# x of batch 2 ahead of the last rows, w2 behind the rows of batch 1, and matmuls into free banks: a cross-attention and feed-forward kernel on one core

## The reference

```
LQ, LKV, HID, H, G = 256, 256, 512, 32, 8      # head size 16, 4 query heads for each of 8 key heads
n = layernorm(x)
q = n @ Wq.T + bq;  k = ctx @ Wk.T + bk;  v = ctx @ Wv.T + bv
scores = q . k / sqrt(16), masked to -inf by a causal_mask argument and by padding
x = x + (softmax(scores) @ v) @ Wo.T + bo
f = layernorm(x)
h = gelu(silu(bitlinear158(f, w1, b1)))         # 512 -> 2048
h = layernorm(h) * ln_g + ln_b
x = x + bitlinear158(h, w2, b2)                 # 2048 -> 512
```

## Time and profile before

| | |
|---|---|
| median of 3 runs | 617.34 us (617.25 to 619.74) |
| the profiled execution | 618.85 us |
| its span, first to last instruction | 616.8 us |
| granted TensorE clock, mean | 0.933 |
| PE, DVE, ACT, POOL busy | 516.5, 490.3, 351.9, 137.9 us |
| moved by DMA | 72.17 MB, 117 GB/s over the span |

### The profile page before, as it was taken

One profiled execution on the slowest core, in us unless ns is written; L12 is line 12 of the kernel. 1 busy time (PEld: TensorE's weight loads), 2 busy tenths in 40 slices (PEclk: granted clock), 3 DMA queues, 4 the chain that ended last, 5 costly groups with the idle time before them and its releaser, 6 DMA issues.

```text
span 616.8 us, 8915 instructions
## 1 busy us (share of the span) xinstructions
PE 516.5 (84%) x3374; PEld 284.2 (46%) x3374; DVE 490.3 (79%) x728; ACT 351.9 (57%) x424; POOL 137.9 (22%) x105
## 2 busy tenths in 40 slices
PE   4927496598989999999999999999959987797656
PEld 4816322364346455645564456445514542333332
DVE  4519972779489988898889889988996899828895
ACT  2204186214865877487648764786468548578721
POOL 5102031110341052105210431131121102403030
PEclk9976889679998999999999999999969997989888
DMA  6797269625621661257125711472126211200000
GB/s 214 238 296 284 92 195 330 186 78 197 145 56 41 200 162 38 75 186 176 37 74 166 192 42 41 162 189 49 40 60 142 62 41 36 53 1 0 35 35 35
DMA packets 32995, 72.17 MB, mean 117 GB/s; under 512 B 7168, under 2 KB 14530, under 8 KB 29951
## 3 DMA queue, kind: packets, MB, share of 16 engines
q1 hardware_dynamic: 31222, 67.06, 37.1%
q0 software_dynamic: 576, 4.19, 2.1%
q10 hardware_dynamic: 1152, 0.31, 0.3%
HBM read 46.50 MB, written 20.61 MB: 109 GB/s over the span
## 4 chain that ended last, share of the span: by engine, by line
PE 56%; DVE 15%; DMA 9%; ACT 8%; issue 7%; POOL 1%; SPq 1%; ACTq 0%; DVEq 0%
PE FF L862 8%; PE PV L802 7%; PE FF L680 6%; PE PV L785 6%; PE FF L911 6%; ACT PT L1083 6%; PE S L769 5%; PE S L743 5%; DVE negm L1356 5%; PE PV L743 2%; DMA denc<-x 2%; PE FF L864 2%; DMA num<-o_raw 2%; DMA x_sb<-in_x 2%; PE FF L876 2%
## 5 line engine op out<-in xcount | busy, mean ns | idle before, releaser
L1083 ACT ACTIVATE PT<-S 128x1024 f32<-128x1024 f32 x128 | 123.6, 1031 | 29.1 <-PE S L769 28.7
L1356 DVE TENSOR_REDUCE negm<-S 128x4 f32<-128x1024 f32 x88 | 105.6, 1214 | 20.8 <-PE S L743 19.1
L769 PE MATMUL S<-Q,K 100*128 100x512 bf16 x256 | 76.3, 404 | 25.4 <-ACT PT L1083 17.4
L743 PE MATMUL S<-K,Q 97*128 97x256 bf16 x352 | 54.8, 282 | 28.3 <-DVE rest L1329 12.9
L862 PE MATMUL FF<-w1t,xqT 128*128 128x512 bf16 x256 | 67.1, 385 | 8.0 <-ACT work L1114 4.3
L785 PE MATMUL PV<-PT,vaug 128*32 128x256 f32 x1024 | 71.9, 401 | 0.6 <-ACT PT L1083 0.6
L802 PE MATMUL PV<-wo_sb,num 128*128 128x512 f32 x128 | 60.9, 621 | 0.7 <-DVE negm L1356 0.6
L1114 ACT ACTIVATE work<-FF,s 128x512 f32<-128x512 f32 x56 | 38.4, 687 | 40.4 <-PE FF L864 40.3
L743 PEld LDWEIGHTS S<-K,Q 97*128 97x128 bf16 x352 | 34.0, 100 | 51.1 <-issue 17.4
L1356 DVE TENSOR_REDUCE negm<-PV 128x4 f32<-128x1024 f32 x40 | 48.8, 1220 | 6.0 <-PE PV L743 5.6
L769 PEld LDWEIGHTS S<-Q,K 100*128 100x128 bf16 x256 | 18.1, 99 | 74.5 <-ACT PT L1083 54.6
(11 more groups left out here) (197 smaller groups left out, 855.9 us busy)
## 6 DMA issues: line engine op xcount, KB each, us to landing
Q<-q_d SPq DMA_DIRECT2D x15, 768.0 KB
q_d<-part SPq DMA_DIRECT2D x8, 768.0 KB, 3.6
x_sb<-in_x SPq DMA_DIRECT2D x8, 512.0 KB, 3.5
ctx_sb<-in_ctxT SPq DMA_DIRECT2D x8, 512.0 KB, 4.0
work<-in_w SPq DMA_DIRECT2D x4, 1024.0 KB, 13.5
q_d<-part SPq DMA_DIRECT2D x8, 512.0 KB, 3.2
xb_sb<-in_x SPq DMA_DIRECT2D x8, 512.0 KB, 4.2
work<-in_w POOLq DMA_DIRECT2D x4, 1024.0 KB, 15.6
```

Of the source, the lines that this page charges most:

```text
L743: last = pe.matmul(to[:, r, :], Q[0:ROWS_1, g, r, t * P:(t + 1) * P], K[0:ROWS_1, g, :], start=not masked, stop=True)
L769: last = pe.matmul(where, K[0:ROWS_2, g, kt * P:(kt + 1) * P], Q[0:ROWS_2, g, 2 * pair:2 * pair + 2, :], start=not masked, stop=True)
L1083: act.activation(PT[:, n % PT_SLOTS, :, :], ST[n % 2][:], ACT.Exp, scale=0.25).then_inc(S["pt_made"], 1)
L1356: dve.tensor_reduce(negm[:, t, R * g:R * g + R], RING_1[n % 3][:], AX.X, ALU.max, negate=True).then_inc(S["max_made"], 1)
```

## The change

- SP issues `load_x(2)` in front of the third group of row loads of batch 0 instead of behind it.
- DVE does `norm_1(2)` behind maximum 1, and `key_rests(1)` in front of all maxima.
- PE does `turn_x(2)` behind score 7 instead of 2, and the pieces of `project_q(2)` behind 8, 10, 12 and 14.
- ACT sums chunk 0 of w1 in front of `turned_x(2)`.
- POOL does `norm_1(3)` and `norm_1_apply(3)` in front of `second_weights`, which now waits for the second half of the rows of batch 1, too.
- DVE does `reciprocal(0)` behind maximum 4 instead of 2.
- PE runs matmuls whose result nobody reads: 7 on `ones` (f32) ahead of everything, 14 behind the scores of step -1 (they wait for maximum 13), 20 behind `weight_sum(0)` in step 0, 6 in step 7, 20 in step 8, and 18 and 10 in step 9. All but the first seven are bf16 on `identb`. All have 512 columns.

```diff
@@ rows_back_first (SP) @@
                 for gs, landed in ((slice(0, 2), "rows_first"), (slice(2, 4), "rows_in0"), (slice(4, 8), "rows_in1")):
+                    if landed == "rows_in1":
+                        load_x(2)
@@ body (SP) @@
                     rows_back_first()
-                    load_x(2)
                     for n in range(1, 4):
@@ second_weights (POOL) @@
                 pool.wait_ge(S["w1_done"], 1)
+                pool.wait_ge(S["rows_in1"], 16 * ROW_LOADS * 2)
@@ body (POOL) @@
-                if at_start(c):
-                    second_weights()
                 if w is not None and w + 1 < B:
                     norm_1(w + 1)
                     norm_1_apply(w + 1)
+                if at_start(c):
+                    second_weights()
@@ PE @@
+            def run_on(bank, count):
+                for _ in range(count):
+                    pe.matmul(bank, identb[:], identb[:].unsqueeze(1).broadcast_to([P, 4, P]), start=True, stop=True)
+
+            def run_up(bank, count):
+                pe.wait_ge(S["c_ones"], 1)
+                for _ in range(count):
+                    pe.matmul(bank, ones[:], ones[:].unsqueeze(1).broadcast_to([P, 4, P]), start=True, stop=True)
@@ body_of (PE) @@
                     weight_sum(c)
+                if at_start(c):
+                    run_on(S1w[:, 0:512], 20)
@@ last_body_of (PE), steps 7, 8 and 9 @@
                     project_out(f, 1, c)
+                    run_on(S1w[:, 0:512], 6)
...
                     layer_2_last(t - 1, 1)
+                    pe.wait_ge(S["xqT_made"], f + 1)
+                    run_on(PVw[:, 0:512], 20)
...
+                        run_on(PVw[:, 0:512], 18 if tok == 0 else 0)
                         turn_hq_last(t, 2 * tok)
                         turn_hq_last(t, 2 * tok + 1)
+                        run_on(PVw[:, 0:512], 10 if tok == 0 else 0)
                         layer_2_last(t, tok)
@@ batches (PE) @@
-                    if n == 2:
+                    if n == 7:
                         turn_x(2)
-                    if n in (5, 8, 11, 14):
-                        project_q(2, [(n - 5) // 3])
+                    if n in (8, 10, 12, 14):
+                        project_q(2, [(n - 8) // 2])
+                pe.wait_ge(S["max_made"], 14)
+                run_on(S1w[:, 0:512], 14)
...
+            run_up(PVw[:, 0:512], 7)
             project_k(0)
@@ body (ACT) @@
+                    weight_abs_sum(0, range(1))
                     turned_x(2)
-                    weight_abs_sum(0)
+                    weight_abs_sum(0, range(1, 4))
@@ body (DVE) @@
-                    norm_1(2)
                     query_rests(1)
-                    maximum(0, 0)
                     key_rests(1)
-                    for n in range(1, 16):
+                    for n in range(16):
                         maximum(0, n)
+                        if n == 1:
+                            norm_1(2)
...
-                    if c is not None and n == 2:
+                    if c is not None and n == (4 if at_start(c) else 2):
                         reciprocal(c)
```

## The result

The changed kernel takes **611.69 us** (median of 4 runs, 611.43 to 612.55), the one before 617.50 in the runs beside it. The ratio is 0.990, with a 95% interval of 0.9875 to 0.9925. So it is faster by about 1%, clear of the noise, as forecast in direction, but by 5.8 us where 19 were predicted; the time lies outside the range of 591 to 606. The profiled execution took 611.71 us, with a span of 609.8 (before: 618.85 and 616.8) and a mean granted clock of 0.950 (before 0.933). That execution of before was 1.5 us above its median, so the spans show 7.0 us gained and the medians 5.8.

The account below looks back on a forecast made before the run. No single engine was taken as the bound; each step has its own. Terms summed to 18.7 us gained: 618.85 to 600.1, less 1.5 for the median 598.6, stated as 598.5, range 591 to 606.

Parts of the forecast that it names:

- the prediction's own signs of being wrong: A wait over 4 us at the division, maxima bound by PE beyond 61, or a fill ending later than its wait.
- Start, 0.8 gained: Seven matmuls on ones first: end near 9, 1.1 us late, but project_k(0) runs at high clock, 1.9 back.
- x of batch 2, 9.8 gained: Batch 0's maxima: x lands at 37.5 to 38.5, last maximum ends 8.5 to 11.4 us before the earlier 69.94.
- 14 matmuls, 0.3 lost: Behind the scores: 3.0 us at high clock against 1.1 of maximum 15 and 1.5 of splitting it.
- 20 matmuls, 1.4 gained: Behind weight_sum(0): 4.4 us inside a 5.4 wait, keeping the clock high into the first exponentials, 18.6 instead of 20.0.
- Wait for the denominators, 9.5 gained: DVE's 9.5 us wait goes entirely, with w2 behind the rows of batch 1 and reciprocal(0) behind maximum 4.
- New wait, 2.5 lost: Reciprocals travel beside w2, so project_out(0, 0) is late: between no wait and 4 to 5 us, middle taken.
- Step 8, 0.7 gained: Twenty matmuls before 581.64 make the 32 transposes high, 3.63 down to about 2 us; DVE's copies then bound.
- Step 9, 0.7 lost: The 18 and 10 matmuls may let the clock fall before the final 16, costing up to 1.7 us.
- that rule 1 in 10: Transposes don't bring the full clock: last transposes count for nothing, step 9 loss 1.7, time 1.0 later, 599.6.
- the waits return behind w2: Rival: reciprocals take the whole 11.2 us and more, PE at low clock in step -1; 604.5 us, chance 0.2.

Follow-up runs that it names:

- branch earlier: Changed kernel with PE's branch on the mask flag taken ahead of the last piece of project_q(1) instead of behind project_v(1), both variants kept: 607.19 us, ratio 0.9833.
- no branch: Changed kernel without PE's branch on the mask flag, the masked variant left out: 604.44 us, ratio 0.980.

## Why the prediction was wrong

The direction was right, and both long waits of DVE went as forecast. What failed is what takes their place: a fetch behind PE's branch that the sum put at nothing, and the reciprocals beside w2, which it put at half. The first was no wait in the rows of before, since a longer one lay over it. All three of the prediction's own signs of being wrong came true: the wait at the division is 4.96 us, PE holds the maxima beyond 61, to 65.96, and the fills at the start end at 10.3, where PE could begin at 7.9 in before. From the profiled executions (those of before and of the change differ by 7.0 us, their medians by 5.8):

| | first score | last maximum | first `scores_2` | last copy | `project_out(0, 0)` | `project_out(6, 0)` | span |
|---|---|---|---|---|---|---|---|
| before | 47.00 | 69.94 | 77.41 | 97.43 | 126.09 | 499.33 | 616.8 |
| after | 40.96 | 65.96 | 74.86 | 95.00 | 118.47 | 491.44 | 609.8 |
| branch earlier | 37.92 | 63.11 | 69.89 | 88.20 | 112.31 | 485.71 | 604.2 |
| no branch | 33.01 | 62.00 | 68.74 | 87.05 | 109.77 | 483.27 | 601.4 |

Term by term, in the prediction's order:

- *Start, 0.8 gained.* 0.3 lost. The 14 records took 9.2 us and ended at 10.3, not near 9; `project_k(0)` then ran high as forecast (1.89). In other runs the same 14 took 7.7 to 9.3, so this term scatters by 1.6 us.
- *x of batch 2, 9.8 gained.* 4.0, the 0.3 of the start taken off already. x landed close to the forecast. The step that failed is "PE is done with keys and values of batch 1 [...] at 34.1, so it has two scores ready". It had their inputs, not their instructions: the first score came at 40.96, 6.56 us after PE's last matmul. Without the branch the first score comes at 33.0 and the maxima end at 62.0, one microsecond beyond the forecast's 57 to 61, so 4 of the missing 5.8 are the fetch. The other 1.9 (62.0 against the 60.1 of the sum) is the first piece of `project_q(2)` at the low clock, for which the text had an upper end of 61.5. PE came to that clock behind DVE's 1.96 us of waiting for x, which the forecast had landing "about when DVE asks".
- *14 matmuls, 0.3 lost.* Nothing: from the last maximum to the write it is 2.22 us, and 2.18 before.
- *20 matmuls, 1.4 gained.* Nothing. "Inside a wait of 5.4" held, but the wait outlasted them by 2.5 us and the clock fell. The price was about right: where the clock stays up, the exponentials take 18.3 instead of 20.0 to 20.1. In the five profiles in which the first exponentials' scores start within 0.5 us of the fills' end, the clock stayed up in three and fell for some microseconds in two. In the eight with 0.8 to 2.5 us between, it fell in all.
- *Not in the sum:* the write of the maxima, 1.5 lost beside an instruction fetch.
- *Wait for the denominators, 9.5 gained.* 9.9.
- *New wait, 2.5 lost.* 5.0, the price at the full 11.2 of its bracket; this term was mis-sized by half. The write and the loads took 7.2 and 5.2 us beside w2, 1.5 and 2.4 to 3.0 without. The middle between two bounds had been taken with no row of its own ("w2 ends at about the same time, which frees the queues"); in fact ACT got w2's last chunk at 113.9, when the reciprocals' loads were about to land too (108.95 plus 5.2). The Trainium skill, "DMA: Bandwidth & Descriptors", section "Queues, rings and completion order", spoke for the full price by its rule that engines alternate between queues, and the trace agrees as far as these lengths go. It also fits that w2 cost the reciprocals nothing where it stood behind them on SP's own queue, with no second queue to alternate with.
- *Step 8, 0.7 gained.* 0.5: the transposes take 1.07 and 1.20 us instead of 3.63 together, with DVE between them.
- *Step 9, 0.7 lost.* 1.4, close to the full price of 1.7. The last transposes ran from 599.35 at the high clock, PE then idled 0.94 us, and from 601 the granted clock is 0.50. In three of the eight profiles with these fills the final 16 ran high all the same. The Trainium skill, "TensorE: Matmul & The Clock Gate", section "Part 4: PE-mode transpose", says that transposes don't bring the full clock, and the text gave that rule 1 in 10. The traces bear it both ways: behind the fills and a wait, the transposes alone did not hold the clock for the final 16 in five of eight profiles, while in before it rose during transposes alone.

Between the columns of the table the spans gain 4.0, lose 1.4 (the write) and 0.1, gain 5.2 (the denominators' wait against the division's), gain 0.3 and lose 0.9 (last steps): 7.0, but for rounding. Of the rivals, "the waits return behind w2" (604.5) was nearest in kind and too small. None had the branch. The chance of 0.96 for faster was borne out.

## What to carry to other kernels

When you take away a wait, ask of the instruction behind it not only when its data come but when its code does. A branch costs an engine a fetch, here 2.5 to 3.1 us of standing still at one place and 6.5 to 8.7 at another, five microseconds later. "Issue" in front of the first instruction behind it and a packet of the instruction queue are its marks. Here it paid to take the branch earlier, where the DMA engines had little to do. And read gains of 1 or 2 us with care: code of another length, even where it isn't run, can put a fetch beside a transfer that is on the path, which took that transfer from 1.5 to 2.9 us here.

## What was not expected of the hardware

- A branch of TensorE costs 2.5 to 3.1 us at 28 to 29 us of this program (six profiles) and 6.5 to 8.7 at 33 to 34 us (eight), where more transfers are under way. The difference lies almost wholly in the time until the packet of instructions begins: 0.1 to 0.4 us against 3.4 to 5.8. That the transfers are the cause fits, but holding some of them back didn't shorten it.
- One instruction fetch of 16 KB beside a write of 48 KB puts its landing from 1.5 to 2.6 to 3.0 us, in nine profiles of nine. The DMA engines were otherwise almost idle (share 0.13 from 68 to 70 us and 0.02 from 70 to 72). That the packet holds up a part of the write behind it is the likely reading, and was not shown.
- Code that is not run moves those fetches: with what 28 matmuls take added to it, they lie at 28, 32 and 56 us instead of 29, 35, 46 and 68. What that is worth in time, two kernels that execute the same do not settle (medians 610.18 and 608.35, with overlapping intervals).
- Filling an idle TensorE is worth little where its end is not that of the wait: all seven places together take PE some 29 us and give 1.4 by the medians. The profiled spans show nothing (609.8 with, 609.2 without), but the one without was the fastest of its four executions.
